# First attention layer: a step's fourth first-pass product is issued behind the values where the step has no job

## What is computed

```python
px = avg_pool_3x3_s2(x)                                   # 28*28 = 784 keys
qt = conv1x1(x, w_qs, b_qs).reshape(B * N_HEAD, D_K, N)   # 3136 queries
kt = conv1x1(px, w_qs, b_qs).reshape(B * N_HEAD, D_K, N2)
vt = conv1x1(px, w_vs, b_vs).reshape(B * N_HEAD, D_V, N2)
q = qt.reshape(B * N_HEAD * m, d, N).transpose(0, 2, 1)   # m = 2 mixtures, d = 8
k2 = kt.reshape(B * N_HEAD * m, d, N2)
attn = jax.nn.softmax(jnp.einsum('bnd,bdk->bnk', q, k2) / temperature, axis=2)
attn = (attn * pi.reshape(-1, 1, 1)).reshape(B * N_HEAD, m, N, N2).sum(1)
out = jnp.einsum('bnk,bvk->bnv', attn, vt)
```

## Time and profile before

| | |
|---|---|
| median of 3 runs | 3918.48 us (3915.25 to 3929.6) |
| profiled execution | 3944.19 us, of it the span from first to last instruction 3942.2 us |
| mean granted TensorE clock | 0.940 |
| TensorE busy | 3749.5 us (95%) |
| VectorE busy | 2739.9 us (70%) |
| ScalarE busy | 2394.8 us (61%) |
| GpSimd busy | 848.9 us (22%) |

### The profile page before, as it was taken

How to read it: one execution, slowest core, us unless ns; L and a number is a source line. 1 busy time by engine, 2 the same in 40 slices (tenths; PEclk the granted TensorE clock), 3 DMA queues, 4 the chain that set the end, 5 groups by cost and what they waited for, 6 DMA issues and landing times.

```text
span 3942.2 us, 70851 instructions
## 1 busy us (share of the span) xinstructions
PE 3749.5 (95%) x27690; PEld 1043.3 (26%) x27690; DVE 2739.9 (70%) x8284; ACT 2394.8 (61%) x2830; POOL 848.9 (22%) x935
## 2 busy tenths in 40 slices
PE   7998899899887999999999999999999999999998
PEld 2222222222222222222222222222222222222221
DVE  5567777777765777766777666777776677777770
ACT  3556766766766256666566666566666656666665
POOL 2143433434525111122101012101112201000000
PEclk6779998989978699999999999999999999999999
DMA  1288888200002023222223222232232222232320
GB/s 51 17 57 56 58 59 55 27 15 19 18 15 72 22 63 92 70 67 70 68 72 82 70 70 70 70 86 74 70 84 79 71 68 70 67 86 74 82 56 26
DMA packets 268053, 236.35 MB, mean 60 GB/s; under 512 B 222184, under 2 KB 225112, under 8 KB 267464
## 3 DMA queue, kind: packets, MB, share of 16 engines
q1 hardware_dynamic: 241544, 205.85, 27.8%
q0 software_dynamic: 26176, 25.98, 3.1%
HBM read 226.65 MB, written 27.19 MB: 64 GB/s over the span
## 4 chain that ended last, share of the span: by engine, by line
PE 80%; DVE 8%; issue 7%; POOL 2%; ACT 2%; DMA 1%; POOLq 0%; SPq 0%; ACTq 0%; DVEq 0%
PE P L731 25%; PE P L716 18%; PE P L684 15%; PE P L697 7%; DVE maxes L1046 7%; PE P L673 5%; PE P L757 4%; PE P L807 2%; PE P L701 2%; PE P L784 1%; POOL high L539 1%; PE P L773 1%; PE P L819 1%; DVE junk L1065 0%; ACT L984 0%
## 5 line engine op out<-in xcount | busy, mean ns | idle before, releaser
L935 ACT ACTIVATE probs<-P 128x896 f32<-128x896 f32 (+1 forms) x2352 | 2117.2, 916 | 1359.2 <-PE P L716 964.2
L1065 DVE CUSTOM_DVE_ANT_0 junk<-P,mstage 112x448 bf16<-112x448 f32 x3136 | 1773.6, 621 | 675.7 <-PE P L684 675.2
L731 PE MATMUL P<-probs,vals 128*17 128x448 f32 (+1 forms) x9408 | 1181.2, 576 | 11.9 <-ACT sums L1011 11.7
L1046 DVE TENSOR_REDUCE maxes<-P 128x1 f32<-128x392 f32 (+1 forms) x1600 | 796.4, 558 | 338.2 <-PE P L673 337.5
L716 PE MATMUL P<-bstage,flip 112*56 112x448 f16 x6272 | 887.1, 363 | 0.0
L684 PE MATMUL P<-keys,q_stack 48*112 48x448 f16 x3136 | 740.2, 400 | 10.6 <-DVE maxes L1065 9.1
L697 PE MATMUL P<-q_two,keys 49*128 49x448 f16 x3136 | 642.2, 352 | 0.0
L684 PEld LDWEIGHTS P<-keys,q_stack 48*112 48x112 f16 x3136 | 284.7, 124 | 887.9 <-DVE maxes L1065 468.0
L673 PE MATMUL P<-keys,q_stack 24*128 24x392 f16 (+1 forms) x1600 | 416.8, 369 | 84.5 <-DVE maxes L1046 52.7
L539 POOL TENSOR_SCALAR high<-projected,cst 128x448 f16<-128x448 f32 x112 | 157.0, 1402 | 1385.0 <-ACT projected L944 1335.2
L716 PEld LDWEIGHTS P<-bstage,flip 112*56 112x56 f16 x6272 | 210.6, 104 | 572.8 <-issue 572.8
(11 more groups left out here) (129 smaller groups left out, 1444.6 us busy)
## 6 DMA issues: line engine op xcount, KB each, us to landing
mstage<-g_max SPq DMA_DIRECT2D x56, 1519.0 KB, 8.0
bstage<-g_bias SPq DMA_DIRECT2D x28, 1568.0 KB, 8.1
bstage<-g_bias SPq DMA_DIRECT2D x28, 1519.0 KB, 7.9
g_max<-t_bf SPq DMA_DIRECT2D x16, 673.8 KB
keys<-d_rden POOLq DMA_DIRECT2D x42, 224.0 KB, 6.0
rwide<-d_rden POOLq DMA_DIRECT2D x42, 224.0 KB, 4.9
g_bias<-t_hi SPq DMA_DIRECT2D x8, 679.9 KB
g_bias<-t_lo SPq DMA_DIRECT2D x8, 679.9 KB
```

The costliest lines, as they stand in the source:

```text
L731: last = mm(P[32 * h:32 * h + HD + 1, PV, 0:QB], table[0:kr, kt, h, :], probs[0:kr, s % 3, h, :], start=kt == 0, stop=kt == unit.tiles - 1 ...
L935: A(probs[0:kr, s % 3, 2 * p:2 * p + 2, :], P[0:kr, 2 * p:2 * p + 2, 0:QB], ACT.Exp).then_inc(exp_done, 1)
L1046: V.tensor_reduce(out=maxes0[0:size, unit.i % 2, t, HALVES[r], c:c + 1], in_=P[0:size, bank_of(job), 0:HALF], op=ALU.max, axis=AX.X).then_ ...
L1065: V.tensor_tensor_reduce(out=junk[:, PLAN.nth[job] % 4, :], in0=P[0:QT, bank_of(job), 0:QB], in1=bias, scale=1.0, scalar=-3.0e38, op0=ALU. ...
```

## The change

Where a step of the first layer has exactly one group, of the first layer, and no job, its fourth product is left out at its old place and issued behind `values(s - 1)`. All other steps keep their order. VectorE's, ScalarE's and GpSimd's programs are unchanged, as is the order in the ring of banks (the values are not in it).

```diff
             for s in range(-PRE, LAST + POST):
+                late = False
...
                         scores(s, 1, False)
                         scores(s, 1)
+
+                    late = inside and len(groups) == 1 and not groups[0][0].biased and not any(PLAN.jobs[s, w] for w in "ab")
                     for g in groups[:1]:
-                        if not g[0].biased:
+                        if not g[0].biased and not late:
                             first_pass0(*g, 3)
...
                 if 1 <= s <= LAST:
                     values(s - 1)
+                if late:
+                    first_pass0(*groups[0], 3)
```

## The result

The changed kernel is slower: 3985.4 us (median of 4 runs, 3968.9 to 3987.9) against 3922.3 us, ratio 1.015 with a 95% interval of 1.012 to 1.019. The forecast was 3913 us in a range of 3882 to 3950. It came out on the side of rival 2, and beyond the 3941 to 3965 us that rival 2 gave.

A forecast was written before the change was run, and what follows sets the result against it. The prediction held that TensorE and VectorE, neither full, hold each other by the ring of three PSUM banks in the first layer. From 3918.48 us, -1.8 by mechanism and -4 by clock gave 3913, range 3882 to 3950.

The forecast's parts named there:

- rival 2: The new loop rules and the clock stays low: 24 to 48 us longer, 3941 to 3965 us; chance 0.21.
- The loop: First-layer cycle of products, scores, values and maxima: lone changed steps gain, every further step in a row costs 0.17 us.
- A lone changed step: Changed step alone between steps with jobs, at 2.4 GHz: it and its successor gain 0.21 us.
- A pair: Two changed steps in a row at 2.4 GHz: gain 0.03 us.
- The round: Third product, scores, values, fourth product, fourth maximum, in changed steps in a row at 2.4 GHz: 2.31 us against 2.14.
- the handover: On TensorE, from last score pair to values at 2.4 GHz: taken as 0.20 us, bounds 0.20 and 0.35.
- a unit's end: Lone step whose group is its unit's last, where VectorE makes the negated maximum: no gain, cost 0.02 us.
- At 1.2 GHz: Changed steps at half clock: a lone step loses 0.18 us, a run of two 0.58.
- The sum by mechanism: All lone steps, pairs and longer runs in the first layer, with the profiled clock unchanged: together -1.8 us.
- The clock: TensorE's time at half speed in the first layer: a few drops less, net -4 us.
- Rival 1: More full speed: 60 to 100 us less at half speed, time 20 to 33 us shorter, around 3890; chance 0.31.
- rival 3: Values don't start earlier, as scores must leave the array first: about +18 us, 3936 us; chance 0.08.

The follow-up runs named there:

- e2: Kernel before, with the fourth product behind the values only in the 89 jobless steps in pairs and longer rows; ratio 1.0109.
- e9: Changed kernel plus one more overwritten issue of the second score pair ahead of the third product in each step behind a bare step; ratio 1.0058.
- e1: Kernel before, with the fourth product behind the values only in the 86 lone jobless steps; ratio 1.0017.
- e3: Changed kernel with the overwritten score pair moved ahead of the third product in every first-layer step; ratio 1.0158.
- e8: Kernel before, with the fourth product behind the values only in the first step of each row of bare steps, lone ones included (126 steps); ratio 1.0072.
- e5: Kernel before, with the second score pair issued once instead of twice in the first layer; ratio 1.0573.
- e6: Changed kernel with the second score pair issued once instead of twice in the first layer; ratio 1.0346.
- e11: Changed kernel with three issues of the second score pair in each step behind a bare one, two of them ahead of the third product; ratio 1.0047.

## Why the prediction was wrong

**The loop: right, one term too small.** A lone changed step with its successor was to gain 0.21 us at 2.4 GHz. Measured between value blocks, with a `q` job behind: 1.53+3.83 = 5.36 against 2.14+3.36 = 5.50, gain 0.13. A pair was to gain 0.03 and loses 0.12 (1.53+2.39+3.83 = 7.75, as in e2 and e9, against 7.63). The round was to be 2.31 and is 2.39. Each time it is the same 0.08, twice in a pair: the handover from scores to values, where no row existed and I took 0.20, is 0.28, inside my bounds of 0.20 and 0.35. The Trainium skill ("TensorEngine Tiling (Array Packing)", Key Properties) says that a change of tiling mode drains TensorE. A score pair gives way to another after 0.20 and to the values over 112 rows after 0.28, which fits, with 0.08 us as the difference; no run separates a drain from the load of the new weights.

At a unit's end I had a loss of 0.02; it is 0.09: the first maximum came 2.61 us after the lone step's first load (646.31 to 648.92), before 2.52. The negated maximum stands ahead of it:

```profile
646.31 0.09 PEld L673 LDWEIGHTS P<-keys,q_stack 24*128 24x128 f16 x1 [0.74 <-issue]
...
648.82 0.22 DVE L1057 TENSOR_REDUCE negmax<-maxes 128x16 f16<-128x32 f32 x1
648.92 0.56 DVE L1051 TENSOR_REDUCE maxes<-P 128x1 f32<-128x392 f32 x1
```

At 1.2 GHz the steps came nearly as reckoned: a lone step's fourth product 2.82 us behind its first (predicted 2.68) and its successor's fourth 4.67 (predicted 4.68), the job 5.21 (predicted 5.11). From value block to value block a lone step loses 0.07 us there, where 0.18 was predicted. The weight loads, first products at 264.02 and 266.84:

```profile
264.02 0.10 PEld L673 LDWEIGHTS P<-keys,q_stack 24*128 24x128 f16 x1 [1.47 <-issue]
...
266.84 0.10 PEld L673 LDWEIGHTS P<-keys,q_stack 24*128 24x128 f16 x2 [1.47 <-DVE maxes L1051]
...
268.69 0.10 PEld L673 LDWEIGHTS P<-keys,q_stack 24*128 24x128 f16 x1 [0.43 <-DVE maxes L1051]
269.23 0.10 PEld L784 LDWEIGHTS P<-q_stack,eye 128*128 128x128 f16 x1 [0.43 <-issue]
```

The sum by mechanism was -1.8 us and the line gives +6.9. That error of 9 us would have left the forecast standing.

**The clock: wrong in sign and more than ten times too small.** The step that failed is "a few drops less ... I take a net of -4 us". It was +54: 166 us more at half speed. The price of that time was right (a third of it), its amount was not. Two readings lie under it, and both failed. The first is of place. I had 18 of the 27 drops begin in the steps that change order, 12 of them in lone ones. I had counted a step from its values to the next values, and the values stand at the end of a step, so the stretch belongs mostly to the step *behind*. Counted from the first load of each step, not one of the 27 began in a bare step: 22 began in the step with a job right behind bare ones (16 behind a lone one, 4 behind a pair, 2 behind three), 15 of these 1.3 to 2.1 us into it, about where its job starts. That is where the change puts the new wait. In the changed kernel it is 13 behind a lone step and 13 behind a pair, of 30. One drop of the changed kernel (loads, then the window of the drop at 618.40):

```profile
616.96 0.09 PEld L673 LDWEIGHTS P<-keys,q_stack 24*128 24x128 f16 x2 [0.74 <-DVE maxes L1051]
...
617.96 0.09 PEld L673 LDWEIGHTS P<-keys,q_stack 24*128 24x128 f16 x1 [0.85 <-DVE maxes L1051]
...
618.43 0.10 PEld L673 LDWEIGHTS P<-keys,q_stack 24*128 24x128 f16 x1 [0.29 <-DVE maxes L1051]
618.96 0.50 PEld L807 LDWEIGHTS P<-keys,wout 128*128 128x128 f32 x2 [0.43 <-issue]
```

```profile
618.40:638.90 20.50, 19.78 (x99) 4.70 (x99) 10.47 (x23) 9.63 (x13) 2.71 (x3) 0.50 0.76 57
```

The step behind the pair begins at 616.96, its third product comes only at 617.96, the fourth at 618.43 and the job at 618.96, already at half clock (its load takes 0.50 us for two instead of 0.30). The clock had fallen at 618.40 and came back 20.5 us later.

One profile stands for each kernel here, so single counts are loose, but behind a pair they go together: 4 before and 3 in e1, which leaves pairs alone; 13 changed, 10 in e2, 13 in e3, 16 in e8; and 4 again in e9, which fills the wait. Before the fall TensorE had done this: values, the first products, then waits for VectorE on the third and fourth product, and behind a lone step on the second too. What the change takes out of a bare step lies where the clock had not fallen.

The second is that I priced *drops*, and their number hardly moved. Of stretches at half speed that begin between 163 and 1300 us the profile of the kernel before has 27, 287 us together; the changed kernel 30 with 369 us, 10 of them of 20 us or more instead of 6; e3 27 with 375 us; e5 29 with 836 us, the longest 191 us. So in these profiles the loss is in how long the clock stays down, more than in how often it falls. e6 goes the other way (53 stretches, 590 us). What keeps it down no run isolates.

**Rival 2** named the right cause, half: that time at half speed would grow. It priced 72 to 143 us, the measured growth is 166. It named the loop as the reason, and e9 says no: it leaves the loop and brings most of the clock back. Longer steps at half speed are too small a reason: a lone step with its successor takes 8.41 instead of 8.34 us there, a pair with its successor 12.12 (in e9) instead of 11.57. By an estimate from these lengths the 403 us would become 406 to 422, and not 569. The price of the unknown could be seen beforehand. The three runs of before spread over 14 us with no change of code, and 96 us hung on time at half speed by my own sum. A range of -31 to +37 us on a term of 96 that no row could bound was too narrow; my bounds for it came from reasons, not from rows.

**Rival 1** fell, **rival 3** was half right (the handover, 0.08 of its 0.15).

**What stays open.** Shown: at a given clock the change costs 7 us, and the rest of its 63 us is time at half speed; one overwritten score pair in the new wait takes nearly two thirds of the loss away; a pair less makes either kernel slower, by 226 and 61 us in the medians. Not shown: which feature of the order the clock answers to. That it is the thin stretch from the end of one value block to the job behind it, 1.53 us before (from 617.15 to 618.68) and 2.01 after (642.48 to 644.49), is my reading. The places of the drops and e9 fit it, but e6 against e5 has the new order better for the clock when less is streamed, e8 has the first step of a row cost three times a lone one, and e11, which moves a pair ahead and adds one, is at 457 us and not below e9's 422. I have no explanation for these that I could show.

## What to carry to other kernels

Where TensorE is neither full nor idle, price an order by two numbers: its time at a given clock, and its time at half speed. Several runs of one kernel with span and granted clock give the line that tells them apart (near the runs that made it), and the spread of the kernel before is the first bound on what a new order may do. Then treat waits of TensorE as something to fill: matmuls whose results are overwritten were worth 5.7% here, and 1.5% lost to a new wait came back to 0.6% with one more pair in it. It saturates: a third issue brought nothing that can be told.

## What the runs showed of the hardware

- Two matmuls of 25 rows by 448 columns per step more or less, which change no step's length at a given clock, decide over 672 us at half speed (1075 against 403) and 226 us of run time.
- TensorE stayed at half clock for 191 us in e5, with 180 us of them recorded busy, and for 51.2 us before with 50.96.
- A score pair on row groups 2 and 3 and a first-pass product on row group 1 run beside each other at 1.2 GHz: a third issue of the pair left the bare step at 3.22 us.
- From a pair of 25-row matmuls to matmuls over 112 rows 0.28 us pass at 2.4 GHz, to another pair 0.20.
